# Transformer on 64 small images: a new order of loads and a warm-up in the patch embedding, and a drain on GpSimd

## What is computed

```python
def _L0_tok_ref(images, W_proj, b_proj, pos_table):
    patches = _patchify(images, PATCH)                  # [64, 36, 768]
    emb = jnp.einsum('bnk,kd->bnd', patches, W_proj) + b_proj
    return emb + pos_table[None, :, :]
...
h = _L0_tok_ref(x, L0_tok_W_proj, L0_tok_b_proj, L0_tok_pos_table)
h = _layernorm(h + _L0_attn_ref(h, L0_attn_W_Q, ...), axis=-1)
h = _layernorm(h + _L0_ffn_ref(h, ...), axis=-1)
h = _layernorm(h + _L1_attn_ref(h, ...), axis=-1)
h = _layernorm(h + _L1_ffn_ref(h, ...), axis=-1)
```

## Time and profile before

| | us |
|---|---|
| median of 3 runs | 911.3 (910.8 to 912.2) |
| the profiled execution | 908.4 |
| its span, first to last instruction | 906.7 |
| TensorE busy in it (matmul) | 819.1 (90%) |
| VectorE busy | 547.4 (60%) |
| ScalarE busy | 460.6 (51%) |
| GpSimd busy | 410.1 (45%) |
| TensorE's granted clock, mean | 0.978 of full |

### The profile page before, as it was taken

How to read it: one execution, slowest core, us unless ns; L and a number is a source line. 1 busy time by engine, 2 the same in 40 slices (tenths; PEclk the granted TensorE clock), 3 DMA queues, 4 the chain that set the end, 5 groups by cost and what they waited for, 6 DMA issues and landing times. The chain is left out here.

```text
span 906.7 us, 20862 instructions
## 1 busy us (share of the span) xinstructions
PE 819.1 (90%) x7501; PEld 738.6 (81%) x7501; DVE 547.4 (60%) x1463; ACT 460.6 (51%) x1150; POOL 410.1 (45%) x489
## 2 busy tenths in 40 slices
PE   5999999999999798997999988898879999999972
PEld 5998998899998477785999976777757999899962
DVE  1335655465556788885773336898876522566654
ACT  1236565556554477784445426878726121355523
POOL 3424443344444444343441225777851455244444
PEclk9999999999999999998999999999989999999996
DMA  8811111011110132213600002633200111333252
GB/s 285 285 31 30 30 37 35 22 35 36 32 39 5 32 57 32 28 24 86 118 1 1 1 27 44 148 59 66 44 4 2 36 63 63 85 104 98 74 178 79
DMA packets 103492, 55.75 MB, mean 61 GB/s; under 512 B 67200, under 2 KB 94192, under 8 KB 103392
## 3 DMA queue, kind: packets, MB, share of 16 engines
q1 hardware_dynamic: 98384, 43.63, 20.1%
q0 software_dynamic: 3792, 7.84, 2.5%
q10 hardware_dynamic: 1216, 2.95, 1.1%
HBM read 29.81 MB, written 13.97 MB: 48 GB/s over the span
## 5 line engine op out<-in xcount | busy, mean ns | idle before, releaser
L931 POOL TENSOR_TENSOR attn_prob<-attn_prob,attn_recip 100x432 f32<-100x432 f32 x64 | 58.6, 915 | 74.8 <-DVE attn_recip L1310 74.5
L450 POOL TENSOR_TENSOR attn_prob_x<-attn_prob,attn_recip 100x864 f32<-100x864 f32 x32 | 52.7, 1646 | 52.5 <-DVE attn_recip L759 52.5
L1886 POOL DMA_INDIRECT results<-moe_hid_shared x43 | 41.4, 962 | 57.7 <-ACT moe_hid_shared L2099 57.7
L1596 ACT ACTIVATE mlp_hid<-psum,columns 128x384 f32<-128x384 f32 x72 | 38.0, 579 | 41.4 <-PE psum L96 41.4
L2461 PE MATMUL psum<-embed_w_tok,embed_patches 128*128 128x192 f32 x216 | 39.6, 346 | 10.7 <-DMA embed_w_tok<-in_tok_w 6.3
L1060 PEld LDWEIGHTS psum<-attn_prob_t,attn_values 108*64 108x64 f32 x1024 | 38.4, 139 | 13.0 <-ACT attn_prob_t L1179 7.7
L2461 PEld LDWEIGHTS psum<-embed_w_tok,embed_patches 128*128 128x128 f32 x216 | 38.0, 203 | 11.8 <-DMA embed_w_tok<-in_tok_w 6.3
L2074 ACT ACTIVATE moe_silu<-psum 128x384 f32<-128x384 f32 x36 | 17.7, 491 | 56.6 <-PE psum L107 56.6
L1060 PE MATMUL psum<-attn_prob_t,attn_values 108*64 108x36 f32 x1024 | 40.7, 225 | 6.2 <-ACT attn_prob_t L1179 3.0
L1033 PE MATMUL psum<-attn_keys_a,attn_q_a 128*64 128x288 f32 x256 | 46.2, 440 | 0.0
L1172 ACT ACTIVATE attn_prob<-attn_prob 100x432 f32<-100x432 f32 x64 | 36.5, 571 | 15.8 <-POOL attn_prob L938 14.9
(11 more groups left out here) (470 smaller groups left out, 2795.9 us busy)
## 6 DMA issues: line engine op xcount, KB each, us to landing
embed_patches<-in_x SPq DMA_DIRECT2D x8, 768.0 KB, 24.1
sorted_rows<-mlp_pad_zeros SPq DMA_DIRECT2D x1, 4214.0 KB, 16.6
moe_hid_shared<-sorted_rows SPq DMA_DIRECT2D x43, 98.0 KB
attn_v<-attn_v_tok SPq DMA_DIRECT2D x16, 216.0 KB
attn_values<-attn_v_tok SPq DMA_DIRECT2D x96, 27.0 KB
side_raw_a<-in_w_gu_dram SPq DMA_DIRECT2D x8, 288.0 KB, 3.3
side_raw_b<-in_w_gu_dram SPq DMA_DIRECT2D x16, 144.0 KB, 3.4
h_rows<-results SPq DMA_DIRECT2D x6, 288.0 KB, 4.9
```

What stands on the lines that cost most here:

```text
L450: nc.gpsimd.tensor_tensor(prob_x[k % 2][:, :, :, :], prob[k % 3][:, :, :].rearrange("p h (a n) -> p h a n", a=1) .to_broadcast([QP, HEADS, ...
L931: nc.gpsimd.tensor_tensor(pr, pr, recip[k % 2][:, :].rearrange("p (h a) -> p h a", a=1) .to_broadcast([QP, HEADS, SEQ]), ALU.mult).then_in ...
L1596: nc.scalar.activation(hid_step(n), bank(n % 3)[:, 0:MW], ACT.Gelu, bias=b_up[:, c:c + 1]).then_inc(S["gelu_done"], 1)
L1886: nc.gpsimd.indirect_dma_start(out=results, out_offset=bass.IndirectOffsetOnAxis(ap=x_in[j % x_ring][:, D:D + 1].bitcast(U32), axis=0), in ...
```

## The change

In the embedding stage:

- SP loads tile 0 in two halves (3 chunks each), then tiles 1, 2 and 3, and only then the bias and the first third of the position table; the other thirds stand between the batches of patches. Each of these small loads counts on the semaphore of the batch behind it: batch 3 also stands for bias and first third, batch 5 for the second third, batch 6 for the last.
- The projection weights are issued by ScalarE, in two halves, at the start. TensorE waits for the first halves before the first 3 matmuls of tile 0 and for the second halves before the other 3.
- ScalarE issues the loads of the four weight jobs one at a time: behind the landing of batch 3, batch 6, batch 7 and batch 8.
- VectorE adds the bias to the table in three pieces, ahead of tiles 0, 3 and 6.
- Before anything has landed, TensorE runs 5 matmuls on a tile that VectorE filled with ones, into a PSUM bank that is free.

In the mixture of experts GpSimd executes a drain behind the last scatter, before its first `add_pair`.

```diff
--- before.py
+++ after.py
@@ -1887,6 +1887,8 @@
                     out=results,
                     out_offset=bass.IndirectOffsetOnAxis(ap=x_in[j % x_ring][:, D:D + 1].bitcast(U32), axis=0),
                     in_=out[j % out_ring], in_offset=None).then_inc(S[f"result_placed{j % signals}"], 16)
+            pool.drain()
+
             def add_pair(i):
                 now = slice(3 * i, 3 * i + 3)
                 pool.wait_ge(S[f"results_loaded{i}"], 32)
@@ -2423,6 +2425,12 @@
         b_tok = sb("b_tok", [P, D])
         stage_a = [sb(f"stage_a{p}", [P, 768]) for p in range(STAGED)]
         stage_b = [sb(f"stage_b{p}", [P, 768]) for p in range(STAGED)]
+        warm = sb("warm", [P, D])
+        half = chunks // 2
+        with_batch = {3: 2, 5: 1, 6: 1}
+
+        def batch_landed(eng, n):
+            eng.wait_ge(S[f"patches_loaded{n}"], 16 + 16 * with_batch.get(n, 0))
 
         def out_bank(t):
             n = t % banks
@@ -2438,26 +2446,42 @@
                 sp.dma_start(patches[:, tiles, :, :], patches_t[tiles].rearrange("t p c n -> p t c n")
                              ).then_inc(S[f"patches_loaded{n}"], 16)
 
-            load(0)
-            sp.dma_start(w_tok[:, :, :], tok_w).then_inc(S["tok_weights_loaded"], 16)
+            def load_pos(k, n):
+                sp.dma_start(pos[:, 3 * k:3 * k + 3, :], pos_rows[:, 3 * k:3 * k + 3, :]
+                             ).then_inc(S[f"patches_loaded{n}"], 16)
+
+            for k in range(2):
+                now = slice(half * k, half * k + half)
+                sp.dma_start(patches[:, 0, now, :], patches_t[0][:, now, :]).then_inc(S[f"half_loaded{k}"], 16)
             load(1)
+            load(2)
+            sp.dma_start(b_tok[:, :], b_rows).then_inc(S["patches_loaded3"], 16)
+            load_pos(0, 3)
+            load(3)
+            load(4)
+            load_pos(1, 5)
+            load(5)
+            load_pos(2, 6)
+            load(6)
             prep["load_columns"](sp)
-            sp.dma_start(pos[:, :, :], pos_rows).then_inc(S["pos_loaded"], 16)
-            sp.dma_start(b_tok[:, :], b_rows).then_inc(S["pos_loaded"], 16)
-            for n in range(2, len(batches)):
+            for n in range(7, len(batches)):
                 load(n)
             prep["load"](sp)
 
         @block.tensor
         def _(pe):
-            pe.wait_ge(S["tok_weights_loaded"], 16)
+            pe.wait_ge(S["warm_ready"], 1)
+            for _ in range(5):
+                nc.tensor.matmul(psum[:, 7 * BANK:7 * BANK + D], warm[:, 0:P], warm[:, :], start=True, stop=True)
             for t in range(NT):
                 for n, batch in enumerate(batches):
-                    if t == batch[0]:
-                        pe.wait_ge(S[f"patches_loaded{n}"], 16)
+                    if n and t == batch[0]:
+                        batch_landed(pe, n)
                 if t >= banks:
                     pe.wait_ge(S["embedded"], t - banks + 1)
                 for c in range(chunks):
+                    if t == 0 and c % half == 0:
+                        pe.wait_ge(S[f"half_loaded{c // half}"], 32)
                     last = nc.tensor.matmul(out_bank(t), patches[:, t, c, :], w_tok[:, c, :],
                                             start=(c == 0), stop=(c == chunks - 1))
                 last.then_inc(S["projected"], 1)
@@ -2467,13 +2491,14 @@
 
         @block.vector
         def _(dve):
-            dve.wait_ge(S["pos_loaded"], 32)
-            nc.vector.tensor_tensor(pos[:, :, :], pos[:, :, :],
-                                    b_tok[:, :].rearrange("p (a n) -> p a n", a=1)
-                                    .to_broadcast([P, POS_TILES, D]), ALU.add
-                                    ).then_inc(S["pos_bias_ready"], 1)
-            dve.wait_ge(S["pos_bias_ready"], 1)
+            nc.vector.memset(warm[:, :], 1.0).then_inc(S["warm_ready"], 1)
             for t in range(NT):
+                if t < POS_TILES and t % 3 == 0:
+                    batch_landed(dve, (3, 5, 6)[t // 3])
+                    nc.vector.tensor_tensor(pos[:, t:t + 3, :], pos[:, t:t + 3, :],
+                                            b_tok[:, :].rearrange("p (a n) -> p a n", a=1)
+                                            .to_broadcast([P, 3, D]), ALU.add).then_inc(S["pos_bias_ready"], 1)
+                    dve.wait_ge(S["pos_bias_ready"], t // 3 + 1)
                 if t == 5:
                     prep["vector_start"](dve)
                 dve.wait_ge(S["projected"], t + 1)
@@ -2485,15 +2510,22 @@
 
         @block.scalar
         def _(act):
-            act.wait_ge(S["tok_weights_loaded"], 16)
-            for j in range(STAGED):
-                load_one(act, S, stage_a, stage_b, jobs, j)
-            for j in range(len(jobs)):
-                round_one(nc, act, S, stage_a, stage_b, jobs, j)
-                if j + STAGED < len(jobs):
-                    load_one(act, S, stage_a, stage_b, jobs, j + STAGED)
-                if j == 2:
-                    following.round(act, S)
+            for k in range(2):
+                now = slice(half * k, half * k + half)
+                act.dma_start(w_tok[:, now, :], tok_w[:, now, :]).then_inc(S[f"half_loaded{k}"], 16)
+            batch_landed(act, 3)
+            load_one(act, S, stage_a, stage_b, jobs, 0)
+            round_one(nc, act, S, stage_a, stage_b, jobs, 0)
+            batch_landed(act, 6)
+            load_one(act, S, stage_a, stage_b, jobs, 1)
+            batch_landed(act, 7)
+            load_one(act, S, stage_a, stage_b, jobs, 2)
+            round_one(nc, act, S, stage_a, stage_b, jobs, 1)
+            round_one(nc, act, S, stage_a, stage_b, jobs, 2)
+            batch_landed(act, 8)
+            load_one(act, S, stage_a, stage_b, jobs, 3)
+            following.round(act, S)
+            round_one(nc, act, S, stage_a, stage_b, jobs, 3)
 
         @block.gpsimd
         def _(pool):
```

## The result

| | before | changed |
|---|---|---|
| median of 22 runs each, us | 911.1 | 906.8 |
| lowest to highest | 905.3 to 915.5 | 904.5 to 911.9 |
| ratio of the runs, changed to before | | 0.9962, interval 0.9944 to 0.9979 |
| profiled execution's span | 906.7 | 908.0 |
| granted clock in it, mean | 0.978 | 0.965 |

The changed kernel is faster: 4.3 us by the medians, 1.9 to 5.1 by the interval. The predicted 907.0 lies 0.2 from the median. Two parts of the change will turn out to gain time: the later weight loads in the embedding, and the drain, which shortens the end of the program.

A forecast was written before the change was run, and what follows sets the result against it. TensorE was taken to bound the kernel, losing 8.5 us in the embedding. The first attention matmul moves from 51.86 to 47.6, 4.3 earlier, drain 0; off the 911.3 median this gives 907.0, range 903.6 to 910.0.

The forecast's parts named there:

- Sharing by packet: Embedding's first transfers: two queues alternate by packet, so the second weight half is in use at 10.0, bounds 6.8 to 13.9.
- rival by bytes: Embedding: queues share by bytes, both weight halves in by 6.8, stage 6.9 earlier, 904.4; chance 0.2.
- The warm-up: Embedding start: 2.8 of matmuls in idle time, yet a clock loss of 1.5 still charged, bounds 0 and 2.0.
- two waits of 2.6 and 2.4: Embedding start: TensorE waits from 4 to 6.6 and from 7.6 to 10.0, around the first half of tile 0.
- TensorE's chain: Embedding: TensorE's matmuls, without further waits after 10.0, end at 46.6, so the next stage starts at 47.6.
- The other chain: Embedding's end: attention 2 weights, issued around 33 to 34, through GpSimd's last subtraction at 44.0; nearly ends the stage.
- Stagger and patches first: Embedding after 10.0: patches arrive with a margin near 4, so the waits of 3.54 and the 3.3 go away.
- Behind the stage: After the embedding's barrier: nothing visible takes the lead of 4.3 back; the rest stays as long as before.
- The drain: GpSimd's drain behind the last scatter: hidden in a 6.05 wait for rows, taken as 0, bounds 0 and some tenths.
- The rival on the other side (late weights): Embedding's end: attention 2 weights land at 51.2, next stage starts at 55.0, 3.1 slower, 914.4; chance 0.05.

The follow-up runs named there:

- the repeat: The changed kernel run once more without further edits, on the same chip as a kernel it was compared with; ratio to before 0.9951.
- one changed line: Against the kernel before, ScalarE's three weight loads wait for batch 3 instead of the projection weights; ratios 0.9943 and, once more, 0.9938.

## Why the prediction came out right, and where its steps were wrong

The time is right, at 906.8 against 907.0, and the place of the forecast gain is right: the embedding's barrier, a lead of 4.3 forecast and 5.3 found. But steps below it compensated each other, and so did the two ends of the kernel. That 4.3 came out to the tenth is luck.

*Sharing by packet* failed. I took the earlier trace rows for a rule and put the second half of the weights at 10.0. They came at 6.2, near the 6.8 of the rival by bytes, though the sharing was not by bytes either. Rows of 2,304 and 3,072 bytes went one for one, rows of 768 bytes went 3.7 to one. The page of the Trainium skill that I set against the row (DMA: Bandwidth & Descriptors, section SWDGE vs HWDGE vs iDMA), with several descriptors in one packet, would allow that; no row shows such a packet, so what sets the share stays open.

*The warm-up* was priced at a loss of 1.5 that did not happen: the data came just as it ended, so there was no wait to lose the clock in, and the pace was the fast one from 4.66 on. Its own length was put at 2.8 and measured 3.56. My two waits of 2.6 and 2.4 were products of the failed step above.

*TensorE's chain* was therefore mis-sized by 4.6 (46.6 against 41.96). The by-bytes rival had 43.9 for it, because it let tile 11 wait for VectorE's bias operations; they took 1.14.

*The other chain* was mis-sized the other way, 44.0 against 46.25, and it is the one that ended the stage. Its failed step: I released the load of the attention 2 weights at the landing of batch 8, 33 to 34. On ScalarE it stands behind the rounding of the value weights, as the rows of the order showed, and was issued at 38.15. That it then took 3.6 and not 10.2 made up for part. Its sum does not close either: 9.4 MB and twice 0.6 are 10.6, not the 12.0 that I used.

*Stagger and patches first.* That the waits go away held. Which part does it I had not asked; the experiments say it is the stagger, and that the table's later place alone gains 0.8. No run has the table's thirds by themselves.

*Behind the stage* I saw nothing that takes the lead back. There was something: TensorE's wait at the barrier, which the change itself made, cost 2.2 by the clock in the profiled run and 0.8 to 2.2 in the others.

*The drain* was the term at 0, with some tenths as the upper bound and only as a cost. I looked at the place where it stands and not at the closing barrier, which waits for a drain of GpSimd too. It costs 0.3 to 1.4 and gains 3.2. So the lead of 4.3 in the runs is not the one that I added up. What reached attention 1 is 3.1 in the profiled run and 3.8 in the repeat. The drain adds about 2 to 3 more, and falls of the clock further back move each execution by several us either way.

The rival on the other side (late weights) had the right mechanism, the wrong size: the weights landed at 42.7, not at 51.2, and 48.1 was where it would have started to cost.

## What to carry to other kernels

When loads that are needed late share the DMA engines with loads that are needed now, let them wait for a landing of the urgent ones; here one such wait gave all of the gain in the embedding, and reordering within a queue only moved the wait. Before crediting an engine with an earlier end, follow every chain into the next barrier in its engine's own order: 8.9 us won on TensorE became 5.3 at the barrier and 3.1 behind it, because an engine that arrives early also waits long enough to lose its clock. A kernel in which the busiest engine arrives last (one changed line, 0.9943 and 0.9938) is as fast as the whole change without having its drain, and stands 2.1 to 2.5 us ahead of it in attention 1. Read the end of the program as well: a kernel whose GpSimd issued indirect DMAs stayed 6.8 at the drain of its closing barrier, and a drain placed where GpSimd mostly waits anyway took 3.2 off the end. The one line together with the drain, and nothing else, was not run.
